# Attention of a vision layer: FP16 transposes from TensorE to transposing transfers, the first normalisation folded into the projection, a new order on every engine

## The reference, cut to what matters

```python
h = einsum('bpk,ek->bpe', patches, W) + b
x = layernorm(h)                       # over the 256 columns
q, k, v = x @ wq, x @ wk, x @ wv       # 256, 64, 64 columns
q, k = rope(q), rope(k)
scores = einsum('bshd,bthd->bhst', q, k) / 4, causal
h = h + (softmax(scores) @ v) @ wo
h = h + ffn_int8(layernorm(h))         # fake quantisation, scales from global maxima
```

## Time and profile before

| | us |
|---|---|
| median of 3 runs | 955.35 (954.17 to 960.56) |
| profiled execution, its own time | 954.55 |
| its span, first to last instruction | 952.8 |

### The profile page before, as it was taken

One profiled execution on the slowest core, in us unless ns is written; L12 is line 12 of the kernel. 1 busy time (PEld: TensorE's weight loads), 2 busy tenths in 40 slices (PEclk: granted clock), 3 DMA queues, 4 the chain that ended last, 5 costly groups with the idle time before them and its releaser, 6 DMA issues. The chain is left out here.

```text
span 952.8 us, 25805 instructions
## 1 busy us (share of the span) xinstructions
PE 820.2 (86%) x8942; PEld 480.8 (50%) x8942; DVE 732.7 (77%) x1309; ACT 621.8 (65%) x972; POOL 520.0 (55%) x545
## 2 busy tenths in 40 slices
PE   2689999999999999999999999999997849997775
PEld 2345555555555555555555555555554433332443
DVE  5856777777777777777777777777777758999898
ACT  3266666666666666666666666666676537886664
POOL 1456666555666566666666665655565326884000
PEclk9789999999999999999999999999999888998899
DMA  7000111111111111111111111111100011322488
GB/s 268 29 2 2 51 57 51 41 39 39 39 39 39 39 39 39 39 39 39 39 39 39 39 50 49 55 39 39 39 13 12 13 43 36 56 44 67 148 261 251
DMA packets 50052, 54.59 MB, mean 57 GB/s; under 512 B 18912, under 2 KB 45280, under 8 KB 50016
## 3 DMA queue, kind: packets, MB, share of 16 engines
q1 hardware_dynamic: 50016, 54.11, 18.8%
HBM read 33.13 MB, written 16.78 MB: 52 GB/s over the span
## 5 line engine op out<-in xcount | busy, mean ns | idle before, releaser
L1223 DVE TENSOR_REDUCE act_all<-pair 128x8 f32<-128x1024 f32 x192 | 235.1, 1225 | 98.6 <-PE pair L532 98.0
L865 ACT ACTIVATE act_all<-pair 128x768 f32<-128x768 f32 x256 | 207.9, 812 | 133.2 <-PE pair L549 133.2
L1013 POOL TENSOR_SCALAR_AFFINE_SELECT act_all<-act_all 128x512 f32<-128x512 f32 x256 | 162.6, 640 | 100.5 <-ACT act_all L865 100.4
L1056 POOL TENSOR_TENSOR act_all<-act_all 128x2 f32<-128x2 f32 x64 | 60.8, 950 | 210.5 <-DVE act_all L1256 139.9
L454 PE MATMUL pair<-act_all 128*128 128x256 f16 (+1 forms) x960 | 118.4, 277 | 9.4 <-DVE act_all L1158 9.4
L857 ACT ACTIVATE act_all<-pair 128x1024 f16<-128x1024 f16 x64 | 65.7, 1027 | 76.7 <-PE pair L509 76.7
L454 PEld LDWEIGHTS pair<-act_all 128*128 128x128 f16 (+1 forms) x960 | 91.5, 99 | 26.6 <-issue 15.4
L525 PE MATMUL pair<-act_all,eye_b 128*128 128x512 bf16 x256 | 78.5, 389 | 26.6 <-DVE act_all L1223 25.9
L563 PE MATMUL pair<-act_all 128*32 128x256 f32 x1024 | 82.7, 395 | 1.3 <-POOL act_all L1013 1.3
L1051 POOL TENSOR_TENSOR act_all<-act_all 128x1280 f16<-128x1280 f32 x31 | 80.9, 2611 | 1.3 <-ACT act_all L795 1.3
L532 PEld LDWEIGHTS pair<-act_all 32*128 32x128 f16 x1536 | 43.4, 93 | 67.3 <-issue 66.0
(11 more groups left out here) (133 smaller groups left out, 1625.9 us busy)
## 6 DMA issues: line engine op xcount, KB each, us to landing
act_all<-x_t SPq DMA_DIRECT2D x32, 640.0 KB, 4.0
out<-act_all SPq DMA_DIRECT2D x32, 256.0 KB, 2.2
ffn<-out SPq DMA_DIRECT2D x16, 512.0 KB, 4.6
out<-ffn SPq DMA_DIRECT2D x16, 512.0 KB, 3.2
act_all<-w_down SPq DMA_DIRECT2D x1, 704.0 KB, 8.4
act_all<-w_emb SPq DMA_DIRECT2D x1, 640.0 KB, 4.0
ffn<-w_gate SPq DMA_DIRECT2D x1, 640.0 KB, 7.1
ffn<-w_up SPq DMA_DIRECT2D x1, 640.0 KB, 7.6
```

Source lines behind the costliest of these rows:

```text
L865: act.activation(probs[:, o:o + 2, 0:3, :].rearrange("p h k s -> p h (k s)"), pair[1][:, :].rearrange("p (h c) -> p h c", h=2)[:, :, 0:3 * P],
L1013: pool.affine_select(out=p, in_=p, pattern=[[0, 4], [1, P]], compare_op=ALU.is_ge, fill=0.0, base=0, channel_multiplier=-1).then_inc(maske ...
L1223: dve.tensor_reduce(to.rearrange("p (g k) -> p k g", g=GROUPS)[:, first:first + 2, :], pair[2][:, :].rearrange("p (k g t) -> p k g t", k=2 ...
```

## The change

- **Transposes.** Every FP16 transpose on TensorE becomes a transposing transfer (`dma_start_transpose`) from SBUF to SBUF on SP's queue: `turn_h` (8 blocks of 128x128), `turn_max` (10), `turn_stack` (6, 6, 4, 4), `turn_on` (8). The PSUM copies behind the old transposes (`max_turned`, `stacked`, `x_turned`, `high_again`) go. The two FP32 `x_turn` and `on_turn` become splits in SBUF plus such a transfer; `o_turn` stays on TensorE.
- **First normalisation.** h itself is split and turned, without normalising. The mean is removed by centring the projection weights once (`centre_weights` on TensorE ahead of its first step, and a correction of `raw_wqkv` on VectorE), and the reciprocal deviation is the scale with which `projected` copies the product out of PSUM. `normalise` goes.
- **Mask.** In diagonal tiles the mask is written after the scores, in four matmuls of 64x64 blocks (64 rows, 64 of the output's partitions, 256 columns) in place of two of 128 rows and 512 columns.
- **Attend.** Two calls of twice the columns in place of four; the probabilities get a second buffer, which lies in the memory of `ffn`, as do the split parts of the attention output. Two stacks.
- **Stack fill.** `fill_stack` makes four small copies in place of one of 1280 columns; `low` does both subtractions; three column groups of `max_stack` that stand for far tiles are set once at the start.
- **Patch** takes one bank, with both halves in it, copied out at once; it and its statistics come one image earlier. Six jobs share the two banks.
- **Steps** run from -3 to 34. All three weights are quantised and turned in step -2.

The new orders of one step x. TensorE: patch(x+3, 0), scores 4 of x-1, units 5 of x, patch(x+3, 1), scores 5, attend 0, scores 6 of x-1, output projection of x-2, units 0 of x+1, scores 7 of x-1, projection 0 of x+2, scores 0 of x, units 1, attend 1 of x-1, units 2, scores 1, projection 1, scores 2, units 3, both `o_turn` of x-1, scores 3, units 4. VectorE: reduction 0 of x+1, variance of x+2, second statistics of x-2, reduction 1, statistics of x+3, reduction 2, low part of h of x+3, reduction 3, sums and normalisation of x-1, reduction 4, low part of the output of x-1, stack fill of x+1, reduction 5, maxima to stack, `low` of x+2, moments of x+3, second normalisation and peak of x-2, residual of x-1. ScalarE: exponential 0 of x-1, o_copy, v, exponential 1, both `projected` of x+1, exponentials 2 and 3, x_high of x+4, high part of the output of x-2, exponential 4, `high` of x+1, exponential 5, copy and high part of h of x+3, exponential 6, o_copy, exponential 7. GpSimd: mask 1 of x-1, the rotation of x+1, masks 2 to 4, x_low of x+4, masks 5 to 7, mask 0 of x, the two powers. SP: load of x+5, turns of h of x+3, output of x-1, maxima operand of x+2, stack of x+1, store of x-2.

```diff
-JOBS = [("patch", 0), ("patch", 1), ("max_t", 0), ("max_t", 1), ("o_t", 0), ("o_t", 1), ("x_t", 0),
-        ("stack_t", 0), ("qkv", 0), ("qkv", 1), ("on_t", 0), ("out", 0)]
-ROLE = {"patch": 2, "x_t": 2, "qkv": 2, "max_t": 1, "stack_t": 1, "o_t": -1, "on_t": -1, "out": -1}
-PER_IMAGE = {"patch": 2, "x_t": 1, "qkv": 2, "max_t": 2, "stack_t": 3, "o_t": 2, "on_t": 1, "out": 1}
+JOBS = [("patch", 0), ("out", 0), ("qkv", 0), ("qkv", 1), ("o_t", 0), ("o_t", 1)]
+PLACE = {("patch", 0): 3, ("out", 0): -2, ("qkv", 0): 2, ("qkv", 1): 2, ("o_t", 0): -1, ("o_t", 1): -1}
+PER_IMAGE = {"patch": 1, "qkv": 2, "o_t": 2, "out": 1}
...
+            def turn_h(n):
+                sp.wait_ge(h_low_ready, n + 1)
+                if n > 0:
+                    sp.wait_ge(done["qkv"], n * 2)
+                sp.dma_start_transpose(h_t.rearrange("p s b c t -> p (s b c) t"),
+                                       h_parts.rearrange("p s e -> p (s e)")).then_inc(h_turned[n % 2], 16)
+            def turn_max(n):
+                sp.wait_ge(high_ready, n + 1)
+                if n > 0:
+                    sp.wait_ge(unit_scored, n * PAIRS_U)
+                sp.dma_start_transpose(max_op.rearrange("p b g t -> p (b g) t"),
+                                       max_stack.rearrange("p b h k -> p (b h k)")).then_inc(max_turned[n % 2], 16)
+            def turn_stack(n):
+                sp.wait_ge(stack_copied, n + 1)
+                sp.wait_ge(low_ready, n + 1)
+                sp.wait_ge(max_ready, n + 1)
+                if n >= 2:
+                    sp.wait_ge(scored, (n - 1) * PAIRS_S)
+                for first, last, turned in ((4, 10, first_turned), (0, 4, second_turned)):
+                    for tb in range(TB):
+                        sp.dma_start_transpose(
+                            qk_op[n % 2][:, first:last, tb * P:(tb + 1) * P],
+                            stacks[n % 2][:, tb, 2 * first:2 * last, :].rearrange("p h k -> p (h k)")
+                        ).then_inc(turned[n % 2], 16)
+            def turn_on(n):
+                sp.wait_ge(on_low_ready, n + 1)
+                if n > 0:
+                    sp.wait_ge(done["out"], n)
+                sp.dma_start_transpose(on_t.rearrange("p s b c t -> p (s b c) t"),
+                                       on_parts.rearrange("p s e -> p (s e)")).then_inc(on_turned[n % 2], 16)
...
                 if p == 0:
-                    pe.wait_ge(read["max_t"], y.n * 2 + 1)
-                    wait(pe, read["stack_t"], y.n * 3)
-                if p == 2:
-                    pe.wait_ge(read["max_t"], y.n * 2 + 2)
+                    pe.wait_ge(max_turned[y.parity], y.half * 16 + 16)
...
-                        pe.matmul(max_bank[j], eye_b[:, :], tri_b.rearrange(
-                            "p (a t) -> p a t", a=1).to_broadcast([P, GROUPS, P]), start=True, stop=False,
-                            skip_group_check=True)
                 for g in range(GROUPS):
                     for j in range(2):
                         kv = 2 * (p % 2) + j
                         rows = slice(32 * kv, 32 * kv + 32)
-                        mm = pe.matmul(max_bank[j][:, g * P:(g + 1) * P], max_op[rows, g, qt * P:(qt + 1) * P],
-                                       max_op[rows, 4, kt * P:(kt + 1) * P],
-                                       start=(qt != kt), stop=True, skip_group_check=True)
+                        mm = pe.matmul(max_bank[j][:, g * P:(g + 1) * P], max_op[rows, qt, g, :],
+                                       max_op[rows, kt, 4, :], start=True, stop=(qt != kt), skip_group_check=True)
+                if qt == kt:
+                    halves = (slice(0, 64), slice(64, 128)) if p % 2 == 0 else (slice(64, 128), slice(0, 64))
+                    for j in range(2):
+                        for t in halves:
...
-            def attend(x, g):
-                pe.wait_ge(masked, x.n * 8 + (2 * g + 2))
-                if g == 0:
+            def attend(x, half):
+                pe.wait_ge(masked, x.n * 8 + (4 * half + 4))
+                if half == 0:
                     pe.wait_ge(v_ready, x.n + 1)
-                if g % 2 == 0:
-                    wait(pe, o_copied, x.n * 2 + (g // 2 - 1))
-                cols = (g % 2) * TOKENS
-                b = o_bank[g // 2]
+                wait(pe, o_copied, x.n * 2 + (half - 1))
+                b = o_bank[half]
                 v = v_aug[x.parity]
+                p = probs[half].rearrange("p (g h) k s -> p g h k s", g=2)
                 for kv in range(KV):
-                    pe.matmul(b[32 * kv:32 * kv + 32, cols:cols + TOKENS], v[:, 0, kv, :],
...
+            def centre_weights():
+                pe.wait_ge(consts_ready, 1)
+                for c in range(DC):
+                    mm = pe.matmul(bank[2][:, 0:QKV_COLS], ones, raw_wqkv[:, c, :], start=(c == 0),
+                                   stop=(c == DC - 1))
+                mm.then_inc(centre_done, 1)
+            centre_weights()
...
+            def embedded(x):
                 z = x + 2
-                act.wait_ge(done["patch"], z.n * 2 + (tb + 1))
+                act.wait_ge(done["patch"], z.n + 1)
                 fence(act)
-                act.activation(h_of(z, tb), shared[JOBS.index(("patch", tb)) % 2][:, 0:D],
+                act.activation(h_of(z), shared[JOBS.index(("patch", 0)) % 2][:, :],
                                ACT.Copy, scale=1.0 / W_UNIT).then_inc(read["patch"], 1)
+                wait(act, h_turned[z.parity - 1], (z + -1).half * 16 + 16)
+                act.wait_ge(read["patch"], z.n + 1)
+                fence(act)
+                act.activation(h_parts[:, 0], h_of(z), ACT.Copy).then_inc(h_high_ready, 1)
...
-                               ACT.Copy, scale=1.0 / W_UNIT).then_inc(read["qkv"], 1)
+                               ACT.Copy, scale=rstd[:, tb:tb + 1]).then_inc(read["qkv"], 1)
...
+            def on_high(x):
                 w = x + -1
-                act.wait_ge(done["on_t"], w.n + 1)
-                wait(act, done["out"], w.n)
-                act.activation(on_t[:, 0].rearrange("p c t -> p (c t)"), shared[JOBS.index(("on_t", 0)) % 2][:, :],
...
-                dve.wait_ge(low_ready, y.n + 1)
-                wait(dve, done["stack_t"], y.n * 3)
-                dve.tensor_copy(stack[:, :, :, 0:32], max_stack).then_inc(stack_copied, 1)
-                dve.tensor_tensor(stack[:, :, HEADS:QK, 32:48], qk[:, :, HEADS:QK, :],
-                                  max_stack[:, :, HEADS:QK, 0:16], ALU.subtract).then_inc(stack_copied, 1)
-            def max_turned(x):
-                y = x + 1
-                dve.wait_ge(done["max_t"], y.n * 2 + 1)
-                wait(dve, unit_scored, y.n * PAIRS_U)
-                dve.tensor_copy(max_op[:, :, 0:P],
-                                shared[JOBS.index(("max_t", 0)) % 2][:, 0:320].bitcast(FP16).rearrange(
-                                    "p (g t) -> p g t", g=5)).then_inc(read["max_t"], 1)
+                z = x + 2
+                stack = stacks[z.parity]
+                dve.wait_ge(high_ready, z.n + 1)
+                wait(dve, first_turned[z.parity], z.half * 32)
+                wait(dve, second_turned[z.parity], z.half * 32)
+                fence(dve)
+                for heads, first in ((slice(0, HEADS), 0), (slice(HEADS, QK), 16)):
+                    for tb in range(TB):
...
+            def h_low(x):
+                z = x + 2
+                dve.wait_ge(h_high_ready, z.n + 1)
+                dve.tensor_tensor(h_parts[:, 1], h_of(z), h_parts[:, 0], ALU.subtract).then_inc(h_low_ready, 1)
```

More of the change, by code:

```diff
@@ L48 @@
 MASKED = -1e30
+FAR = 60000.0
 W_UNIT = 64.0
@@ L376, in _ @@
+            for n in range(FIRST_STEP, IMAGES + 3):
+                step(Image(0, n))
             for k in range(2):
@@ L425, in _, with take_bank @@
         def _(pe):
[L426 removed]
+            def take_bank(img, job):
                 at = JOBS.index(job)
[L429 to L430 removed]
+                x, back = img + -PLACE[job], 2
+                while back < 4 * len(JOBS):
                     turn, place = divmod(at - back, len(JOBS))
                     kind, nth = JOBS[place]
[L433 to L435 removed]
+                    last = x + (PLACE[JOBS[place]] + turn)
+                    if last.exists():
+                        wait(pe, read[kind], last.n * PER_IMAGE[kind] + (nth + 1))
                         break
                     back += 2
[L438 to L439 removed]
                 return shared[at % 2]
@@ new lines, in step @@
+                if (x + -1).exists():
+                    exp_pair(late, 4)
+                if (x + 1).exists():
+                    high(late)
+                if (x + -1).exists():
+                    exp_pair(late, 5)
+                if (x + 3).exists():
+                    embedded(early)
+                if (x + -1).exists():
+                    exp_pair(late, 6)
+                    o_copy(late, 0)
+                    exp_pair(late, 7)
```

(7 more changed lines are left out.)

630 lines of the change are left out of this document (266 added, 364 removed).

## The result

| | before | after |
|---|---|---|
| median us | 954.76 (952.71 to 960.56, 4 runs) | 899.51 (895.74 to 903.28, 4 runs) |
| profiled execution, its span | 954.55, 952.8 | 903.28, 901.6 |
| one image in the loop | 22.64 | 20.06 |

The ratio is 0.9419, with a 95% interval of 0.939 to 0.9449. The change is faster by 5.8%; the prediction was 803 us in a range of 772 to 885. The direction is right, the size is not: 899.5 lies 14.5 us above the range.

The account below looks back on a forecast made before the run. TensorE (16.7 us) and VectorE (16.5) share the bound; with 1 us for backlog the period is 17.5 us per image. 28 periods plus 313.2 us for start, end and feed-forward make 803 us, range 772 to 885.

Parts of the forecast that it names:

- three filling steps: Pipeline start: three steps without full work, projection, rotation, high part and turn in series, costing 16.0, 16.0 and 16.2 us.
- images 3 to 31: Attention loop: 28 periods of 17.5 us, 1 us less for the first step without a patch.
- tail to the last peak's end: Attention's end behind image 31's unit pair: reductions, turns, scores, product and residual to the peak, 42 us.
- so 16.5 us if it never waits for anyone: VectorE's list per image: 16.0 us busy plus about 0.5 of its own pauses.
- (a): Loop from maximum to scores: stack transfers land at 17.8 us, scores are due at 17.9; no slack.
- (b): Loop from high part to units: the turn lands at 15.6 us, the first unit pair is due at 15.7; no slack.
- rival B: SP's queue becomes the bound: period towards 21.7 us, time to 921; with half that, 19.6 and 862. Chance 0.27.
- the DMA prices: SP's transposing transfers: 8 blocks hold SP 1.23 us, land in 3.1; engines busy 11.6 us per image.
- the TensorE sum: TensorE's work left per image after the transposes go: 16.7 us, from 15.5 to 18.1.
- Rivals C: Slower: nothing on the queue overlaps a transposing transfer, load and store neither; period 27.9 us, 1094 us. Chance 0.04.
- E: The change buys little: an unforeseen wait of 4 to 5 us in each image, 921 to 965 us. Chance 0.03.
- D: Slower: granted clock falls; mean under 0.73 makes 16.7 into 22.9, fully lower level over 1200 us. Chance 0.04.

Follow-up runs that it names:

- Experiments 5: The changed kernel with GpSimd's low part of x cut into five pieces of 256 columns between the masks: 870.93 us.
- 6: The changed kernel with GpSimd subtracting only 8 of 1280 columns for the low part of x from the third image on: 874.0 us.
- 7: The changed kernel with the stack fill moved from VectorE to ScalarE and GpSimd's low part of x in five pieces: 827.89 us.
- 10: The changed kernel with GpSimd computing the low part of x twice, one after the other: 998.23 us.
- (9): The kernel before the change with GpSimd's low part of x in five pieces of 256 columns: 953.28 us.
- experiments 4: The changed kernel with one more transposing transfer of 8 blocks per image, ahead of the maximum operand's turn: 937.98 us.
- 11: fill_act_pieces with one more transposing transfer of 8 blocks per image, ahead of the maximum operand's turn: 883.49 us.
- fill_act_pieces: The kernel of experiment 7: the changed kernel with the stack fill on ScalarE and the low part of x in five pieces: 827.89 us.
- xlow_later: The changed kernel with GpSimd's low part of x moved, in one piece, from behind mask 4 to behind mask 0: 923.13 us.

## Why the prediction was wrong, and where it was right

Laid out by the prediction's own sum, from the profile of the changed kernel (903.3 us; a unit pair's end is taken as the start of VectorE's first reduction of the image):

| term | predicted | measured |
|---|---|---|
| first unit pair ends | 48.3 | 48.28 |
| three filling steps | 48.2 | 64.8 (19.8, 20.8, 24.2) |
| images 3 to 31 | 28 x 17.5 - 1 = 489 | 565.0 = 28 x 20.18 |
| tail to the last peak's end | 42 | 49.7 |
| feed-forward and rest | 175.7 | 175.6 |

**The step that failed** is the one before the rivals: "so 16.5 us if it never waits for anyone", with ScalarE and GpSimd put down as lying "beneath". VectorE's list without stands is 16.3 by the measured rows, so its work was priced well; but VectorE and GpSimd do not run independently, and VectorE is busy 19.3 us per image, 3.8 of it stands. 76 of the 100 us of error are in the 28 images. Experiments 5, 6, 7 and 10 show the cause from both sides: cut the long instruction and the period falls by 1.0 us; double it and it rises by 4.0, 2.6 of that as busy time of VectorE and the rest with a lower clock. The cut gives back 1.0 of the 2.6 us between 20.06 and 17.5; for the rest the stands that stay (rotation, masks) are read from the rows, and no experiment took them away alone. The prediction had a view that showed it and did not read it so: GpSimd's 14 us were compared with a total, and no row was asked whether an instruction of VectorE takes longer beside GpSimd. It named a rival for the queue, for the transfers and for the clock, and none for an instruction that lasts longer than its price. In the loop the trace of before shows it only in the two durations of one shape (9), but its start showed it plainly (order of time of the kernel before; L1264 is `normalise`, L1180 a scale of six columns):

```profile
17.21 2.60 POOL L1051 TENSOR_TENSOR act_all<-act_all 128x1280 f16<-128x1280 f32 x1
17.29 3.00 DVE L1264 TENSOR_SCALAR act_all<-act_all 128x256 f32<-128x256 f32 x2 [0.88 <-POOL act_all L1056]
...
24.53 0.17 DVE L1180 TENSOR_SCALAR w_scale<-w_scale 128x6 f32<-128x6 f32 x1
...
29.11 1.52 POOL L1021 TENSOR_TENSOR act_all<-act_all 128x640 f32<-128x640 f32 x1
29.45 1.23 DVE L1180 TENSOR_SCALAR w_scale<-w_scale 128x6 f32<-128x6 f32 x1
```

Two normalisations, 0.61 each in the loop by the earlier trace rows, take 3.00 there, and the scale of six columns has two durations, 0.17 and 1.23, the longer one up to the end of GpSimd's instruction.

**The layout of the loops** (a) and (b) was right, and experiments 4 and 11 confirm that they have next to no slack. From the end of the stack write to the first score the trace has 418.18 to 422.52, 4.34 us, for which the prediction had 4.8. That is also why the stands cost time on the way to the scores too: merge and stack write are links of loop (a), and the fill is the start of loop (b), where ScalarE waits 2.9 us per image for it:

```profile
ACT act_all L825 <- DVE act_all L1186: 28.9, 10, 3.0
```

(waits of the changed kernel, 300 to 508 us). The sign that I had set for rival B, over 1.5 us of waits for a DMA, came true at 2.0 us, without B being the cause: TensorE waits for the transfer last, but the transfer took its predicted time and was started late, and VectorE, which fills the period, waits for TensorE 0.2 us in 200.

**Right**: the DMA prices (8 blocks were to hold the queue 1.23 us and land in 3.1, and in the changed kernel the turns of h and of the output did both; DMA share 0.53 at a period of 20.06, as 11.6 us would give 0.58), the TensorE sum (16.7 against 16.85), the mask (0.33 each) and, a little low, the product (2.6 against 2.9), the first unit pair. Rivals C and E did not occur, and of D only a stretch before the loop: the clock is 1.00 between 300 and 500 us.

**Wrong in size**: the filling steps, 16.6 us too short, and the tail, 7.7. Part of that is the same stands (in the first image the fill's first two copies take 4.1 us), part a granted clock of 0.74 between 60 and 100 us, which I had taken as full. In fill_act_pieces, with fewer stands and at a clock of 0.99 in the same stretch, the three steps took 47.54 to 99.29, 51.8 us. How the 16.6 divides between the two causes is open. These two terms also decide on which side of the range the time fell: 28 steps of 20.18 with the predicted start and end make 313.2 + 565.0 = 878 us, inside the range, whose upper part had been meant for the queue. So the range would have covered the step by luck, for another mechanism.

## What to carry to other kernels

A sum per engine holds only if the engines are independent: look for the same instruction with two durations in one trace, and at what ran beside the longer one. Where VectorE is the bound, try cutting GpSimd's long instructions into pieces between its short ones, rather than moving them; moved, the one here hit another instruction, and taking work off VectorE first can bring nothing until the pieces are there. An engine's slack under the old bound is cover for such stands, and a change that removes the old bound removes it.

## What the runs showed of the hardware

A VectorE instruction of 2 columns out of and into SBUF took 2.49 us, one of 32 columns (FP32 to FP16) 2.63, both beside one instruction of GpSimd of 2.62; alone they take 0.16 and 0.24. Both read one tensor, in SBUF, and write to SBUF. `affine_select` on GpSimd makes VectorE stand too, while reductions out of PSUM kept 1.21 to 1.23 us beside it. A reduction out of SBUF did not stand either (changed kernel, start; the two low parts of x end at 24.01, and the scale of six columns behind the reduction ends with them, 0.67 us long in place of 0.17):

```profile
18.38 5.63 POOL L1007 TENSOR_TENSOR act_all<-act_all 128x1280 f16<-128x1280 f32 x2 [17.87 <-ACT act_all L797]
21.62 1.72 DVE L1147 TENSOR_REDUCE w_scale<-ffn 128x6 f32<-128x1536 f32 x1
23.37 0.67 DVE L1148 TENSOR_SCALAR w_scale<-w_scale 128x6 f32<-128x6 f32 x1
```

Alone the reduction takes 1.75. Not every instruction of GpSimd makes VectorE stand: in the kernel before a copy of 1280 columns starts at 419.43 beside a power of two columns (419.42, 0.69 us) and takes 0.52, against 0.49 elsewhere. Batch statistics, whose input lies in SBUF, didn't stand either: in xlow_later two of them took 0.74 us in the middle of a low part of x, as they do elsewhere (order of time of that kernel):

```profile
67.60 2.61 POOL L1007 TENSOR_TENSOR act_all<-act_all 128x1280 f16<-128x1280 f32 x1
...
68.25 0.74 DVE L1231 BATCH_NORM_STATS2 act_all<-act_all 128x6 f32<-128x256 f32 x2
```

It goes the other way as well: the sum of the rotated halves takes 1.54 us in the changed kernel, where it starts first, and 2.02 in fill_act_pieces, where VectorE's low part (0.69 us) started 0.08 us ahead of it:

```profile
411.91 0.69 DVE L1290 TENSOR_TENSOR ffn<-act_all,ffn 128x512 f16<-128x512 f32 x1 [0.20 <-ACT ffn L863]
411.99 2.02 POOL L1019 TENSOR_TENSOR act_all<-act_all 128x640 f32<-128x640 f32 x1
```

Back-to-back transposing transfers overlap: the stack's four are issued in 5.16 us and each lands in 2.7 us by the median, so latency is hidden but the issue is not.
